# A Mamba mixing stage laid out with states and channels together on the partitions, the convolution moved to TensorE

## The chip, the cores and the metric

One core of one Trainium2 chip runs the kernel; seven cores stand idle. The metric is device time in microseconds (us) of one execution. The kernel before was timed three times, and one further execution was profiled.

## The reference, cut to what matters

Two residual layers over x [8, 512, 256]. Layer 0 (attention and experts) is not touched. Layer 1, for each of the 8 batches:

```python
xn = _layernorm(x, axis=-1)
x, z = split(einsum('bld,ed->ble', xn, in_proj_w))        # 512 channels each
u = silu(causal_conv_4_taps(x) + conv1d_b)
x_dbl = einsum('bld,rd->blr', u, x_proj_w)                # dt_low 16, B 16, C 16
delta = softplus(einsum('blr,dr->bld', dt_low, dt_proj_w) + dt_proj_b)
h[t] = exp(delta[t] * A) * h[t-1] + delta[t] * B[t] * u[t]      # 512 channels x 16 states
y[t] = sum_n(h[t] * C[t]) + u[t] * D_param
out = einsum('bld,ed->ble', y * silu(z), out_proj_w)
x = x + out + ffn(xn)     # ffn: 256x256 product, both sides rounded to a 6-bit grid in blocks of 32
```

## The kernel before

`route_block` and `attend_block` do layer 0. They end near 1025 us of the span and are the same in both kernels. `mix_block` does layer 1, and the whole change lies in it.

**The pieces.** The recurrence of a batch has 4 chunks of 128 channels (on the partitions), 16 states and 512 times. It is cut into 32 pieces; a piece is one chunk and two states, so a tile of 128x1024. Each piece q passes through four engines. ScalarE (ACT) makes the decays exp(delta*A) into one of three PSUM slots (`decay`, L1250, two instructions at L1257). GpSimd (POOL) makes the inputs B*du into one of `WS` = 6 slots of `work` (`drive`, L1148). VectorE (DVE) runs the scan in PSUM (`scan`, L1372) and multiplies the state of the piece before by C (`read`, L1378). TensorE (PE) adds the two halves of `work` into the bank of y with the identity as weights (`sum_states`, L1481).

**What holds what.** `decay` of piece n waits for `read` of piece n-3. `drive` of piece n waits until piece n-WS is summed, since it takes its slot:

```python
if n >= WS:
    pool.wait_ge(summed, n - WS + 1)
```

DVE's order is scan(q), the step work of q, read(q-1). PE's order at q is the step work of q, then the sum of piece q-1. At the end of a chunk, `gate_y` (L1386) multiplies y by silu(z) on DVE; it waits until PE has summed the whole chunk, and it stands behind the scan of pieces 1, 9, 17 and 25. `seed` (L1476) then opens the bank of y again with u*D.

**Step work of the next batch.** Between the pieces of batch b the engines prepare batch b+1. The constants `PE_AT`, `ACT_AT`, `DVE_AT` and `POOL_AT` (L62 to L67) name the piece at which each step stands. In their order: gather and weigh the expert rows (POOL, L1077, L1083), add them to x (L1088), layer norm (DVE L1327 to L1334, POOL L1092 to L1102), transpose (PE L1456), x half of the input projection (PE L1461), the last tap and the bias (ACT L1208), the other three taps (DVE L1363, in `convolve`), silu (ACT L1214), B, C and dt_low (PE L1467, ACT L1220), delta (PE L1471, ACT L1224 to L1231, POOL L1136 to L1140), z (PE L1461, ACT L1235, L1239), rounding to the grid (DVE L1341 to L1354, POOL L1111 to L1129), output projection of batch b-1 (PE L1489 to L1494, ACT L1247), cut in eight parts over pieces 2 to 9.

**The copies over the partitions.** B and C are rows of one partition each, wanted on all 128. SyncE's queue (SP) stores the 32 rows to memory (L1035) and loads them back as eight broadcasts of 1 MB, one for each pair of states (L1043). They are needed again only at the next batch, and each is loaded when the last piece of its kind is done.

## Time and profile before

| | |
|---|---|
| median of 3 runs | 2258.15 us (2257.34 to 2266.96) |
| profiled execution, its own time | 2259.47 us |
| its span, first to last instruction | 2257.7 us |
| TensorE clock granted, mean | 0.926 of 2.4 GHz |
| DVE, PE, POOL, ACT busy over the span | 1582.8, 1794.6, 1052.2, 963.1 us |

The span is 1.8 us shorter than the execution's own time. PE is the engine with the most busy time over the whole span, but layer 0 and layer 1 have different limits, so each is read for itself.

### The profile page before, as it was taken

The numbers are of one execution on the slowest core, as the hardware profiler recorded it, in microseconds if no ns is written. First come the engines' busy times: TensorE is split into PE (matmuls) and PEld (weight loads), VectorE is DVE, ScalarE is ACT, GpSimd is POOL, SyncE is SP. The second block draws the span as 40 slices with busy tenths as digits, with TensorE's granted clock in tenths as the row PEclk, the third lists the DMA queues.
The fourth block names the chain that finished last, engine by engine and source line by source line (L and its number), as shares of the span: only waits on it lengthen the run. The fifth ranks groups of instructions, "written<-read, shape, count | busy, mean of one in ns | idle before, by whom it ended". The sixth has DMA issues, their size and how long they took to land.

```text
span 2257.7 us, 20924 instructions
## 1 busy us (share of the span) xinstructions
PE 1794.6 (79%) x6312; PEld 844.5 (37%) x6312; DVE 1582.8 (70%) x1836; ACT 963.1 (43%) x1480; POOL 1052.2 (47%) x740
## 2 busy tenths in 40 slices
PE   7489899989899989894368877787777777877876
PEld 7253535353535353531123423433234233342333
DVE  6456464646464646452598898988979889889895
ACT  3125252626252525352437346364363643735532
POOL 2600000000000000004878959879598796896962
PEclk9899999999999999996689988999899998999999
DMA  5553536253526262602402204003031040210400
GB/s 179 205 80 109 92 101 100 101 96 106 93 98 103 94 107 94 107 10 82 159 0 81 98 1 159 19 32 128 19 142 37 1 158 19 99 70 2 149 10 9
DMA packets 84205, 189.13 MB, mean 84 GB/s; under 512 B 10561, under 2 KB 62914, under 8 KB 72370
## 3 DMA queue, kind: packets, MB, share of 16 engines
q1 hardware_dynamic: 81074, 180.07, 29.0%
q0 software_dynamic: 3072, 8.37, 1.2%
q8 instruction: 25, 0.41, 0.1%
q14 instruction: 34, 0.28, 0.0%
HBM read 151.72 MB, written 36.70 MB: 83 GB/s over the span
## 4 chain that ended last, share of the span: by engine, by line
DVE 14%; PE 11%; POOLq 11%; POOL 10%; issue 6%; ACT 1%; DVEq 1%; ACTq 0%
DVE ps L1372 6%; PE ps L1481 6%; DVE work L1378 3%; POOLq L1120 3%; POOL work L1148 3%; POOLq L1196 2%; POOL xn L1124 2%; PE ps L1461 2%; DVE u L1363 2%; POOLq L1139 2%; POOLq L1137 2%; PE ps L1489 2%; POOL e_rows L1122 1%; DVE absmax L1345 1%; POOL e_rows L1083 1%
## 5 line engine op out<-in xcount | busy, mean ns | idle before, releaser
L1481 PE MATMUL ps<-work,ident_sb 128*128 128x512 f32 x1024 | 548.0, 662 | 210.5 <-DVE work L1378 209.9
L1148 POOL TENSOR_TENSOR work<-bc,du 128x1024 f32<-128x1024 f32 x256 | 601.4, 2361 | 181.3 <-PE ps L1481 179.4
L1372 DVE TENSOR_TENSOR_SCAN ps<-ps,work 128x1024 f32<-128x1024 f32 x256 | 585.4, 2287 | 93.9 <-ACT ps L1257 50.4
L1257 ACT ACTIVATE ps<-delta,a_neg 128x512 f32<-128x512 f32 x512 | 331.7, 682 | 318.3 <-DVE work L1378 317.6
L699 DVE TENSOR_REDUCE m<-ps 128x1 f32<-128x512 f32 x512 | 327.3, 685 | 164.0 <-PE ps L805 162.3
L1481 PEld LDWEIGHTS ps<-work,ident_sb 128*128 128x128 f32 x1024 | 200.1, 208 | 500.0 <-DVE work L1378 321.1
L622 ACT ACTIVATE prob<-ps 128x1024 f32<-128x1024 f32 x256 | 256.8, 1021 | 234.5 <-PE ps L829 232.3
L1378 DVE TENSOR_TENSOR work<-ps,bc 128x1024 f32<-128x1024 f32 x256 | 308.4, 1205 | 0.0
L563 POOL TENSOR_TENSOR m_parts<-m,nil 128x16 bf16<-128x16 f32 x32 | 7.1, 221 | 604.2 <-DVE m L699 604.2
L805 PE MATMUL ps<-k_st,q_st 96*128 96x512 bf16 x512 | 184.5, 407 | 59.0 <-DMA k_st<-qk_parts 36.9
L1461 PE MATMUL ps<-xn_t,in_w 128*128 128x512 f32 x256 | 142.0, 688 | 54.0 <-DVE u L1363 35.1
L771 PE MATMUL ps<-rows_t,w 128*128 128x320 f32 x512 | 166.7, 470 | 4.3 <-ACT rows_t L600 4.3
L829 PE MATMUL ps<-q_st,k_st 99*128 99x512 bf16 x512 | 148.1, 383 | 0.1
L840 PE MATMUL ps<-prob,v 128*32 128x512 f32 x1024 | 139.8, 619 | 0.1
L577 POOL TENSOR_TENSOR att<-att,x_res 128x1024 f32<-128x1024 f32 x8 | 18.8, 2345 | 244.4 <-DVE att L684 244.4
L805 PEld LDWEIGHTS ps<-k_st,q_st 96*128 96x128 bf16 x512 | 48.1, 99 | 209.4 <-DVE m L699 137.1
L780 PE MATMUL ps<-w,hid 128*128 128x256 f32 x512 | 118.7, 382 | 5.9 <-ACT hid_rest L604 5.7
L771 PEld LDWEIGHTS ps<-rows_t,w 128*128 128x128 f32 x512 | 104.4, 208 | 46.7 <-issue 10.9
L671 DVE COPY e_out<-ps 128x256 f32<-128x256 f32 x32 | 12.0, 417 | 138.0 <-PE ps L780 138.0
L780 PEld LDWEIGHTS ps<-w,hid 128*128 128x128 f32 x512 | 95.8, 190 | 27.1 <-ACT hid_rest L604 11.2
L603 ACT ACTIVATE hid<-ps 128x256 f32<-128x256 f32 x128 | 49.2, 384 | 132.6 <-PE ps L771 132.6
L1461 PEld LDWEIGHTS ps<-xn_t,in_w 128*128 128x128 f32 x256 | 52.4, 214 | 135.2 <-issue 58.1
(168 smaller groups left out, 2045.3 us busy)
## 6 DMA issues: line engine op xcount, KB each, us to landing
bc<-bc_rows SPq DMA_DIRECT2D x64, 1024.0 KB, 4.7
w<-in_w SPq DMA_DIRECT2D x32, 1024.0 KB, 8.6
qk_parts<-parts SPq DMA_DIRECT2D x96, 128.0 KB
q_st<-qk_parts SPq DMA_DIRECT2D x96, 128.0 KB, 10.5
k_st<-qk_parts SPq DMA_DIRECT2D x96, 128.0 KB, 11.3
dispatch<-zeros SPq DMA_DIRECT2D x4, 1280.0 KB, 10.6
x_in<-in_x SPq DMA_DIRECT2D x8, 512.0 KB, 3.6
rows<-dispatch SPq DMA_DIRECT2D x32, 128.0 KB, 7.3
```

Source lines behind the costliest of these rows:

```text
L622: nc.scalar.activation(prob[:, n % PB, :, :], ps[:, ST[n % 2]:ST[n % 2] + 2, :], ACT.Exp, scale=SCALE).then_inc(prob_ready, 1)
L699: nc.vector.tensor_reduce(m[:, g % 2, qt, 2 * pair + i:2 * pair + i + 1], ps[:, S0 + i, :], AX.X, ALU.max).then_inc(s_reduced, 1)
L771: x = nc.tensor.matmul(ps[:, HIDE[i] + h % 2, 0:CAP], w1[:, i, k, h * P:(h + 1) * P], rows_t[:, k, :], start=(k == 0), stop=(k == KD - 1))
L780: x = nc.tensor.matmul(ps[:, E_OUT[i], j * DM:(j + 1) * DM], hid[:, h, j * P:(j + 1) * P], w2[:, i, h, :], start=(h == 0), stop=(h == HC - 1))
L805: nc.tensor.matmul(ps[:, S0 + i, :], q_st[0:STACK, h, qt * P:(qt + 1) * P], k_st[0:STACK, h, :], start=True, stop=True).then_inc(s_done, 1)
L829: x = nc.tensor.matmul(ps[:, ST[n % 2] + i, :], k_st[0:STACK + MROWS, h, kt * P:(kt + 1) * P], q_st[0:STACK + MROWS, h, :], start=True, st ...
L1148: nc.gpsimd.tensor_tensor(work[:, n % WS, :, :], bc[:, j, 0, :, :], du[:, b % 2, c, :].unsqueeze(1).broadcast_to([P, PAIR, SEQ]), ALU.mult ...
L1257: e = nc.scalar.activation(state(n)[:, i, :], delta[:, b % 2, c, :], ACT.Exp, scale=a_neg[:, c, PAIR * j + i:PAIR * j + i + 1])
L1372: nc.vector.tensor_tensor_scan(s, s, work[:, n % WS, :, :].rearrange("p i t -> p (i t)"), 0.0, ALU.mult, ALU.add).then_inc(state_ready, 1)
L1378: nc.vector.tensor_tensor(work[:, n % WS, :, :], state(n), bc[:, j, 1, :, :], ALU.mult).then_inc(read_ready, 1)
L1461: x = nc.tensor.matmul(ps[:, bank, :], in_w[:, k, col:col + P], xn_t[:, k, :], start=(k == 0), stop=(k == KD - 1))
L1481: x = nc.tensor.matmul(ps[:, YB, :], sb["ident"][:, :], work[:, n % WS, i, :], start=False, stop=(n % PAIRS == PAIRS - 1 and i == PAIR - 1))
```

## The change

A piece now holds 4 states times 32 channels on the partitions, for two blocks of 32 channels side by side: again 128x1024, again 32 pieces a batch, 8 to a chunk. delta and du of 32 channels must then stand on four groups of 32 partitions, so they are stored to memory and loaded back by SP (`store_inputs`, `load_inputs`); B and C need a quarter of the room. `sum_states` uses weights of 32 columns (`pick`, four stacked identities), so that each half of a piece goes to its own 32 output partitions. The convolution goes into the input projection: `tap_weights` multiplies the projection's weights by each tap once, and `in_proj_taps` adds 4 shifted products. Weighing and normalising go from POOL to ACT, two scalings of the grid go from POOL to ACT, `WS` falls from 6 to 4, and the steps get other places.

```diff
-PAIR = 2
-PAIRS = NS // PAIR
-PIECES = DC * PAIRS
-WS = 6
+CH = 32
+BLOCKS = P // CH
+QUADS = NS // BLOCKS
+PIECES = DC * QUADS * BLOCKS // 2
+PER_CHUNK = PIECES // DC
+WS = 4
 XS = 3
+US = 6
 RESET = 1e35
-GRID_STEPS = 5
+GRID_STEPS = 3
...
-PE_AT = {"out": 2, "w": 2, "first_quant": (3, 4), "turn_x": (10, 11), "x": (12, 13, 14, 15), "bc": 18, "dt": (19, 20, 21, 22),
+PE_AT = {"out": (1, 3), "w": 1, "first_quant": (3, 4), "turn_x": (6, 7), "x": (8, 10, 12, 14), "bc": 17, "dt": (19, 20, 21, 22),
          "z": (23, 24, 25, 26), "turn_quant": (27, 28)}
...
+ACT_AT = {"out": (4, 6), "w": 2, "first_quant": (4, 5), "weigh": 0, "normalise": 6, "turned": (8, 9), "x": (11, 13, 15, 17), "silu_u": 17,
+          "step": 13, "rows": 19, "dt": (21, 22, 23, 24), "softplus": 24, "z": (25, 26, 27, 28), "quant": (29, 30), "silu_z": 30}
+DVE_AT = {"statistics": 2, "max": 7, "binade": 10}
+POOL_AT = {"add": 1, "root": 5, "down": 10, "grid": 15, "up": 18, "gather": 20, "input": 27}
...
+                def load_quad(f, k):
+                    if f:
+                        sp.wait_ge(read_ready, f * PIECES - PER_CHUNK + 2 * k + 2)
+                    rows = io["bc"][f % 2].rearrange("(n r) t -> n (r t)", r=2)
+                    for i in range(QUADS):
+                        n = QUADS * k + i
+                        sp.dma_start(bc[i * CH:(i + 1) * CH, k, :, :].rearrange("p r t -> p (r t)"),
+                                     rows[n:n + 1, :].broadcast_to([CH, 2 * SEQ])).then_inc(bc_loaded[k], 16)
+
+                def store_inputs(f, c):
+                    sp.wait_ge(du_ready, f * DC + c + 1)
+                    sp.dma_start(io["rep"][f % 2, c], inputs[:, c, :, :].rearrange("p r t -> p (r t)")).then_inc(rep_stored[c], 16)
+
+                def load_inputs(f, c):
+                    sp.wait_ge(rep_stored[c], f * 16 + 16)
...
+                    for i in range(QUADS):
+                        sp.dma_start(rep[i * CH:(i + 1) * CH, c, :, :, :].rearrange("p j r t -> p j (r t)"),
+                                     io["rep"][f % 2, c].rearrange("(j p) x -> p j x", p=CH)).then_inc(rep_loaded[c], 16)
+
+                def spread(f):
+                    store_rows(f)
+                    store_inputs(f, 0)
+                    store_inputs(f, 1)
+                    load_inputs(f, 0)
+                    store_inputs(f, 2)
+                    load_inputs(f, 1)
+                    load_quad(f, 0)
+                    store_inputs(f, 3)
+                    load_quad(f, 1)
+                    load_inputs(f, 2)
+                    load_quad(f, 2)
+                    load_quad(f, 3)
+                    load_inputs(f, 3)
...
+                    if q % PER_CHUNK == 0:
+                        pool.wait_ge(rep_loaded[c], (b + 1) * QUADS * 16)
+                    if c == 0 and h == 0:
+                        pool.wait_ge(bc_loaded[k], (b + 1) * QUADS * 16)
                     if n >= WS:
                         pool.wait_ge(summed, n - WS + 1)
...
+                def scale_step(f):
+
+                    act.wait_ge(step_ready, f + 1)
+                    if f:
+                        act.wait_ge(rep_stored[DC - 1], f * 16)
+                    nc.scalar.activation(nudge, xn_step[:, :, :], ACT.Copy, scale=-2.0 ** -22)
+                    nc.scalar.activation(xn_step[:, :, :], xn_step[:, :, :], ACT.Copy, scale=1.5 * 2.0 ** 20).then_inc(step_scaled, 1)
...
-                    nc.vector.tensor_reduce(absmax[:, :], blocks(xn[:, :, :]), AX.X, ALU.max, apply_absolute_value=True)
+                    nc.vector.tensor_reduce(absmax[:, :, 0], blocks(xn[:, :, :]), AX.X, ALU.max, apply_absolute_value=True)
...
-                    nc.vector.tensor_scalar(xn_step, xn_step, 1.0, 4.0, ALU.max, ALU.min).then_inc(step_ready, 1)
-
-                def convolve(f, c, bank):
...
+                    cross = xn_step[:, :, :].rearrange("p t c -> p (t c)").rearrange("p (c i) -> p i c", i=2)
+                    nc.vector.tensor_scalar(cross, cross, 1.0, 4.0, ALU.max, ALU.min).then_inc(step_ready, 1)
...
+                def in_proj_taps(bank, c, done):
+
+                    for s in range(TAPS):
+                        for k in range(KD):
+                            x = nc.tensor.matmul(ps[:, bank, s:], in_x[:, k, TAPS - 1 - s, c * P:(c + 1) * P], xn_t[:, k, 0:SEQ - s],
+                                                 start=(s == 0 and k == 0), stop=(s == TAPS - 1 and k == KD - 1))
+                    x.then_inc(done, 1)
...
                     pe.wait_ge(read_ready, n + 1)
-                    for i in range(PAIR):
-                        x = nc.tensor.matmul(ps[:, YB, :], sb["ident"][:, :], work[:, n % WS, i, :],
-                                             start=False, stop=(n % PAIRS == PAIRS - 1 and i == PAIR - 1))
+                    for i in range(2):
+                        j = 2 * (n % 2) + i
+                        x = nc.tensor.matmul(ps[j * CH:(j + 1) * CH, YB, :], pick[:, :], work[:, n % WS, i, :],
+                                             start=False, stop=(n % PER_CHUNK >= PER_CHUNK - 2))
                     x.then_inc(summed, 1)
...
+                            for h in range(HALVES):
+                                if q == PE_AT["out"][h]:
...
+                                    out_proj(b - 1, h)
```

Before the first batch, POOL also gathers the expert rows of the second batch ahead of its `scale_input`, and PE waits for `tap_weights`. In the loop, PE's `in_proj_taps` of chunk c waits until ACT has taken chunk c-1 out of the bank (`in_taken`), and the output projection stands in two unbroken halves at pieces 1 and 3.

## Rows read from the trace of the kernel before

**Rows 1.** Page: busy times over the span.
```profile
PE 1794.6 (79%) x6312; PEld 844.5 (37%) x6312; DVE 1582.8 (70%) x1836; ACT 963.1 (43%) x1480; POOL 1052.2 (47%) x740
```

**Rows 2.** Busy time by stretch: length; PE, PEld, DVE, ACT, POOL; PEclk, DMA share, GB/s.
```profile
60.00:1024.00 964.00, 847.12 (x4000) 413.43 (x4000) 516.18 (x920) 382.64 (x641) 89.64 (x174) 0.95 0.44 99
1085.00:1090.00 5.00, 0.00 (x0) 0.00 (x0) 4.02 (x7) 2.82 (x2) 2.44 (x3) 0.50 1.02 431
1485.75:1631.43 145.68, 113.54 (x265) 48.76 (x264) 126.92 (x94) 69.74 (x100) 117.73 (x68) 0.92 0.19 69
```

**Rows 3.** Waits of DVE from 1140 us on: total, times, longest.
```profile
DVE ps L1372 <- ACT ps L1257: 49.1, 20, 4.0
DVE ps L1372 <- POOL work L1148: 31.3, 22, 2.6
DVE u L1363 <- ACT u L1208: 15.9, 14, 2.1
DVE sz L1386 <- PE ps L1481: 15.7, 17, 2.7
```

**Rows 4.** Timeline of DVE: start us, us, engine, line, operation, tiles, idle before.
```profile
1475.11 2.37 DVE L1363 SCALAR_TENSOR_TENSOR u<-ps,conv_w,u 128x509 f32<-128x509 f32 x3
...
1499.59 2.28 DVE L1372 TENSOR_TENSOR_SCAN ps<-ps,work 128x1024 f32<-128x1024 f32 x1
1502.90 2.28 DVE L1372 TENSOR_TENSOR_SCAN ps<-ps,work 128x1024 f32<-128x1024 f32 x1
...
1513.63 2.30 DVE L1372 TENSOR_TENSOR_SCAN ps<-ps,work 128x1024 f32<-128x1024 f32 x1 [4.01 <-ACT ps L1257]
```

**Rows 5.** Timeline of PE: 32-column tiles, sums, projection, an output half's ends.
```profile
400.45 1.06 PE L840 MATMUL ps<-prob,v 128*32 128x512 f32 x8
...
1478.66 3.11 PE L1481 MATMUL ps<-work,ident_sb 128*128 128x512 f32 x4 [3.04 <-DVE work L1378]
...
2100.15 1.88 PE L1481 MATMUL ps<-work,ident_sb 128*128 128x512 f32 x4
2101.86 1.88 PE L1461 MATMUL ps<-xn_t,in_w 128*128 128x512 f32 x4
...
2237.09 1.99 PE L1489 MATMUL ps<-out_w,sz 128*128 128x256 f32 x8 [0.79 <-DVE sz L1386]
...
2244.34 0.70 PE L1494 MATMUL ps<-x,ident_sb 128*128 128x256 f32 x2
```

**Rows 6.** Groups of POOL and ACT in one batch, 1485.75 to 1631.43 us.
```profile
L1148 POOL TENSOR_TENSOR work<-bc,du 128x1024 f32<-128x1024 f32 x32 | 74.9, 2357 | 23.0 <-PE ps L1481 22.7
L1124 POOL TENSOR_TENSOR xn<-xn,e_rows 128x1024 f32<-128x1024 f32 x3 | 7.1, 2355 | 0.5 <-issue 0.5
L1138 POOL TENSOR_TENSOR du<-delta,u 128x512 f32<-128x512 f32 x4 | 5.1, 1268 | 0.6
L1077 POOL DMA_INDIRECT e_rows<-expert_out,slot_cur x4 | 4.0, 999 | 1.6 <-issue 1.6
...
L1257 ACT ACTIVATE ps<-delta,a_neg 128x512 f32<-128x512 f32 x64 | 41.5, 682 | 37.1 <-DVE work L1378 36.9
```

**Rows 7.** Two lines of DVE, all their instructions: ns min/median/max.
```profile
L1345 DVE TENSOR_SCALAR absmax<-absmax x8: 180/4066/4586, 1053.4 to 2027.6; 128x32 f32<-128x32 f32 x8
...
L1354 DVE TENSOR_SCALAR e_rows<-e_rows x7: 693/2667/2673, 1194.0 to 2067.2; 128x1024 f32<-128x1024 f32 x7
```

**Rows 8.** Timeline of the stage's start.
```profile
1037.20 3.64 POOL L1083 TENSOR_SCALAR e_rows<-e_rows,gate_cur 128x256 f32<-128x256 f32 x4 [5.90 <-DMA e_rows<-expert_out,slot_cur]
...
1047.22 4.85 POOL L1102 TENSOR_SCALAR xn<-x,moments,rstd 128x256 f32<-128x256 f32 x4 [0.18 <-issue]
...
1054.87 16.29 PE L1461 MATMUL ps<-xn_t,in_w 128*128 128x512 f32 x32 [0.78 <-ACT xn_t L1203]
...
1087.91 1.26 POOL L1136 TENSOR_TENSOR delta<-delta,du 128x512 f32<-128x512 f32 x1 [2.42 <-ACT du L1231]
...
1100.47 2.34 POOL L1148 TENSOR_TENSOR work<-bc,du 128x1024 f32<-128x1024 f32 x1
```

More of the change, by code:

```diff
@@ L967, in mix_block @@
         fw_step = sz[:, 1, 1, :].rearrange("p (h c) -> p h c", h=2)
-        xn_step = e_rows[:, :, :].rearrange("p (h t) c -> p h (t c)", h=2)
+        xn_step = e_rows
+        conv_rows = work[:, 0:2, :, :].rearrange("p a i t -> p (a i) t")
+        nudge = inputs[:, DC - 1, :, :].rearrange("p r (t d) -> p (r t) d", d=DM)
+        delta, du = inputs[:, :, 0, :], inputs[:, :, 1, :]
         const_loaded = sem("const_loaded3")
@@ L1163, in _ @@
                 scale_up(0)
+                pool.drain()
+                place_gather(1)
+                gather(1, range(TT))
                 for c in range(DC):
@@ L1197, in _, with weigh_experts, normalise @@
                                 scale_input(f, c)
+                        if f + 1 < BATCH:
+                            if q == POOL_AT["gather"]:
+                                pool.drain()
+                                place_gather(f + 1)
+                                gather(f + 1, range(2))
+                            if q == POOL_AT["gather"] + 1:
+                                gather(f + 1, range(2, TT))
             @block.scalar
             def _(act):
+                def weigh_experts(f):
+                    act.wait_ge(e_gathered, (f + 1) * TT * 16)
+                    for t in range(TT):
+                        r = nc.scalar.activation(e_rows[:, t, :], e_rows[:, t, :], ACT.Copy, scale=gate_cur[:, t:t + 1])
+                    r.then_inc(e_weighed, 1)
+                def normalise(f):
+                    act.wait_ge(rstd_ready, f + 1)
+                    if f:
+                        act.wait_ge(quant_turned, f * KD)
+                    for t in range(TT):
+                        r = nc.scalar.activation(xn[:, t, :], x2[:, f % XS, t, :], ACT.Identity, scale=rstd[:, t:t + 1], bias=shift[:, t:t + 1])
+                    r.then_inc(xn_ready, 1)
                 def copy_turned(f, k, bank):
@@ L1303, in _ @@
                             silu_u(f)
-                        if q == ACT_AT["bc"]:
+                        if q == ACT_AT["step"]:
+                            scale_step(f)
+                        if q == ACT_AT["rows"]:
                             copy_rows(f, TB)
@@ L1362, in convolve, with tap_weights @@
+                def tap_weights():
+                    dve.wait_ge(const_loaded, CONSTS * 16)
+                    raw = in_x[:, :, TAPS - 1, :]
+                    for tap in range(TAPS):
+                        if tap == TAPS - 1:
                             dve.drain()
-                        r = nc.vector.scalar_tensor_tensor(u[:, f % 2, c, s:], ps[:, bank, 0:SEQ - s], conv_w[:, c, k:k + 1],
-                                                           u[:, f % 2, c, s:], ALU.mult, ALU.add)
@@ L1418, in _ @@
                 block_scale(0)
-                for c in range(DC):
-                    convolve(0, c, 2 + c)
                 binade(0)
```

286 lines of the change are left out of this document (132 added, 154 removed).

## The prediction

> **What bounds the kernel now.** I read the page first: over the whole span PE has the most busy time [rows 1], but the change lies in the second half. The busy time of one batch of the mixing stage says more [rows 2]: in 145.7 us DVE works 126.9, POOL 117.7 and PE 113.5. The timeline of DVE shows why: two scans follow each other after 3.31 us [rows 4], so 32 pieces are 106 us of every batch. The waits of DVE [rows 3] are what is left: in seven batches it waited 49.1 us for ACT's decays, 31.3 for POOL's drives, 15.9 and 15.7 in the convolution and the gate. DVE bounds the stage, with 18.8 us of waits a batch, and the reader should see that each other engine has time left on average. What counts is whether it delivers on time.
>
> **How much lateness the loop bears after the change.** With four slots in `work`, drive n starts when piece n-4 is summed, and takes 2.36 us [rows 6]. Read n-4 ends 0.1 after scan n-2 has begun. A sum then takes about 1.0: the 32-column tiles of the attention stage do four products side by side in 1.06 [rows 5], where the two of a piece now take 1.88 one after the other [rows 5]. So the sum is done 1.1 after scan n-2, and is needed 6.6-2.4 = 4.2 after it. The room is about 3 us; with hand-overs I use 2.8. Whatever stands on PE ahead of a sum, or on POOL beside its drives, costs DVE what exceeds it.
>
> **The terms of one period** (one batch; seven of eight have them, the last one in part).
>
> 1. DVE's own work. The convolution goes: 4 x 2.37 [rows 4] = 9.5. The scaling of 32 maxima takes 4.07 beside a working POOL and 0.18 at the stage's start, and the clamp of the steps 2.67 against 0.69 [rows 7]. Both now read with a stride of two. Nothing in the trace shows that form; the scaling can cost 0.18 to 4.07. I take 0.18, because only these forms, which take 0.69 for 1024 elements when left alone [rows 7], show the long times, and I expect the strided form to lose that pace: minus 3.9. The rule speaks against this. The Trainium skill, "Vector Engine (DVE) Microarchitecture Reference", section 5.1, lists for the mode with both ports a single source in SBUF and an even outer dimension, and no stride; by it the wait stays, and the total is 27 us more. DVE's work: 126.9-9.5-3.9 = 113.5.
>
> 2. Output projection in two unbroken halves. One half runs from 2237.09 to 2245.04 = 7.95 us [rows 5]. At piece 1 PE starts it after the gate, 2.9 us after the scan began, then come the seed 1.0, as two passes cost half of a pair [rows 5], and the sum of piece 0: done at 12.9, drive 4 at 15.3. DVE would be there at 12.1 (three pieces of 3.31, some 2.2 for the gate and the statistics): it waits 3.2. The second half at piece 3 does it again, 3.3. Together 6.5.
>
> 3. The taps on PE. A product of 128x512 is two passes of 0.43 (1.72 from one row to the next for four [rows 5]); `in_proj_taps` has 16, so 7.1 us with its tail, ahead of the sums 7, 9, 11 and 13. Block one starts 2.0 after scan 8 (ACT copies the transposes at 8 and 9), sum 7 is done at 10.3, and the gate behind scan 9 has stood since 6.2: 4.1. Block two waits until ACT, at its piece 11, has taken chunk 0: it starts 2.3 after scan 10, sum 9 ends at 10.5, drive 13 at 12.9, and DVE came at 11.7: 1.2. Blocks three and four: PE needs 7.1+2.3 for two pieces for which DVE needs 6.6: 2.8 each. Together 10.9.
>
> 4. POOL at 15 to 21: three grid steps and scaling up at 2.5 each with the drain, the gathers 5.6 [rows 6]. That is 15.6 beside seven drives that leave 0.95 each: 15.6-6.7-2.8 = 6.1. Gone are weighing and normalising; they stood where POOL had its room or waited already, so their going is in the new count, which replaces the old 31.3/7.
>
> 5. ACT: softplus keeps its 4.0 [rows 4]; the gate of piece 25 waits 1.2, as the z product ahead of sum 23 waits for ACT. The other ACT waits fall into those of 3 and 6. The steps that ACT takes over (eight of 128x256 and two of 128x1024, by its 682 ns for 512 [rows 6] some 5.5 us) fit between decays; it is busy 69.7 of 145.7 [rows 2]. If that cover is gone, they cost up to 5.
>
> 6. POOL at 27 to 30: four inputs of 2.9 (2 x 1.27 [rows 6] and drains) = 11.6, minus 5 x 0.95 and the room of 1.5 that the z products leave: 5.4.
>
> Terms 2 to 6 are waits of 34.1; the period without the next term is 147.6.
>
> 7. The reload, which is new. Drive 0 of a batch needs `rep` of chunk 0 and quad 0 of B and C, and ahead of them in SP's order stand the stores of chunks 0 to 2 and the loads of chunk 1. Counted from the second input (its store releases the first load): 1.05 MB of stores and 4.72 MB of loads. Whole-partition loads ran at 431 GB/s; the attention stage, whose loads fill few partitions, moved 99 GB/s at a share of 0.44, so 225 when full [rows 2]. The new loads fill 32 partitions each. Narrow: 21.0+2.4+1 for issue = 24.4; wide: 14.4. POOL itself needs 12.9 more for its remaining inputs and drives, and DVE has 0.9 of room. The wait is 1 to 11; I take 11, as the narrow row is the nearer one. The Trainium skill, "SBUF — State Buffer", Door 1, says 32 partitions reach 8 of 16 ports, 189 GB/s for 1 MiB, and that loads to different groups don't add up; by its rate the estimate is a wait of 15 and a total of 28 us more.
>
> Period: 158.6, against 145.7: +12.9, seven times = +90.
>
> **The start.** PE began the projection at 1054.9 and the first drive stood at 1100.5 [rows 8]. Weighing and normalising on ACT save 3.64+4.85 less about 3: 5 earlier. The taps add 48 passes: +20.6; the convolution they replace ran beside PE. `scale_step` ahead of delta: +2.4. POOL does grid and the second gather before its inputs, 15.6 after `scale_step` where ACT needs some 13: +2.6. Then the reload, with nothing beside it: the inputs start at 1108.5, the second ends at 1114.3, +24.4 gives 1138.7: 38 later; wide 28.
>
> **The last batch** has term 2 and a shorter last sum: +5.5.
>
> **The sum:** 90+38+5.5 = 133 on the profiled 2259.5 us; the median stands 1.3 lower: **2391 us**. Unknown as well: the clock. The granted clock was 0.92 in a batch [rows 2]. A sum took 3.11 behind a PE wait of 3.04, and 1.88 behind other products [rows 5]: the lower level, 1.2 of 2.4 GHz. PE now works a third of each quiet piece; if all four late blocks (two halves, the first taps, z) start so, 1.2 each is 34 in total. I put in 0, the value of blocks that follow each other, and keep 34 for the range. This case alone spans 2310 to 2440.
>
> **The rivals.**
> - **The blocks are hidden, and DVE's saving comes through (faster).** Against it is the step-by-step count above; for it, PE's total falls, to 113.5-32 x 0.9+20.6 = 105 a period, so there is room on average. It decides at one place: the sum behind a block of taps must be done by 4.2 us after scan n-2. Then ACT and POOL waits stay at 7.0 and 4.5 [rows 3] and the reload at 1: 126.0 a period, 7 x -19.7 = -138, start +28: **2150 us**.
> - **The loads run at the wide rate.** Everything else as above: -70-10: **2311 us**. Against it is the row at 0.44.
> - **The two 32-column products don't overlap.** A sum stays at 1.88, and each of six blocks lets go 0.9 later: +40: **2431 us**. Against it is the row of 1.06, though that one has four tiles; for it, that none has two.
> - **Savings and blocks cancel.** Wide loads, and POOL's terms half hidden: near 2260.
>
> **How the numbers follow.** Forecast with its own bounds 0.50, wide loads 0.14, no overlap 0.08, cancelling 0.08, hidden blocks 0.20. I read a difference of over 0.5% (11 us) as one that measurement can tell. Faster 0.20, and of the cancelling case most is same: 0.05; slower 0.75. The range leaves out most of the faster case and a little at the top: 2240 to 2445.
>
> **What would show it.** Right: DVE's scans wait for POOL's drives after pieces 3, 5, 12, 14 and 16, and POOL for PE; the gate of piece 9 waits 4 us; the first drive of each batch waits for a DMA on `rep` or `bc` by about 10; the sum of a piece takes about 1.0; the first scan stands near 1141. Wrong: a period near 126 with no DMA wait at the seam, a scaling of maxima still at 4, or sums at 1.9.

## The result and the profile after

The changed kernel takes **2435.41 us** (median of 4 runs, 2432.92 to 2437.33) against 2257.74 us of the kernel before on the same chip (2256.93 to 2266.96): a ratio of 1.078, 95% interval 1.076 to 1.080. It is 178 us slower. The prediction had 2391 us in a range of 2240 to 2445, and slower at 0.75: direction and range held, and 44 us are missing.

The page after, first the busy times of the span, then the row of the copies (KB each, median us from issue to landing):

```profile
PE 1817.2 (75%) x6696; PEld 770.0 (32%) x6696; DVE 1505.5 (62%) x1744; ACT 1001.6 (41%) x1542; POOL 941.8 (39%) x676
...
rep<-rep_rows SPq DMA_DIRECT2D x128, 512.0 KB, 16.0
```

Against [rows 1], DVE and POOL did less (77 and 110 us), PE 23 us more. No engine is nearer to its limit than it was, so the 178 us are waits. One batch by itself, and two stretches in which the loads ran (columns as in [rows 2]: length; PE, PEld, DVE, ACT, POOL; PEclk, DMA share, GB/s):

```profile
1637.36:1800.50 163.14, 112.13 (x312) 38.47 (x312) 118.07 (x81) 75.21 (x108) 104.14 (x61) 0.79 0.37 88
1613.00:1618.00 5.00, 1.92 (x4) 0.19 (x4) 3.05 (x3) 2.56 (x3) 4.58 (x5) 0.50 1.04 208
1643.00:1655.00 12.00, 11.39 (x43) 7.40 (x43) 9.99 (x14) 4.36 (x7) 3.48 (x2) 0.83 1.04 216
```

DVE's work fell by 8.9 us a batch (126.92 to 118.07) and the batch grew from 145.7 to 163.1. What DVE waited for, from 1140 us on, answers to [rows 3]:

```profile
DVE ps L1440 <- POOL work L1181: 282.4, 86, 38.3
DVE sz L1454 <- PE ps L1555: 42.4, 15, 3.6
DVE ps L1440 <- ACT ps L1316: 36.2, 13, 5.0
```

Waits for ACT fell from 49.1 to 36.2 and those of the convolution (15.9) are gone. Waits for the gate rose from 15.7 to 42.4, waits for POOL's drives from 31.3 to 282.4. Of these, 38.3 lie ahead of the first scan, which here comes after 1140 us and in the kernel before came ahead of it; like is compared with like at 31.3 and 244.1. The timeline of DVE in one batch shows where the drives are late: at the first scan, at piece 4, at piece 6, from 15 to 21 and from 29 on; the gate of piece 9 is the one that waits for PE.

```profile
1637.36 2.30 DVE L1440 TENSOR_TENSOR_SCAN ps<-ps,work 128x1024 f32<-128x1024 f32 x1 [13.59 <-POOL work L1181]
...
1657.65 2.30 DVE L1440 TENSOR_TENSOR_SCAN ps<-ps,work 128x1024 f32<-128x1024 f32 x1 [4.57 <-POOL work L1181]
...
1666.55 2.30 DVE L1440 TENSOR_TENSOR_SCAN ps<-ps,work 128x1024 f32<-128x1024 f32 x1 [2.17 <-POOL work L1181]
...
1676.70 2.16 DVE L1414 TENSOR_SCALAR absmax<-absmax 128x32 f32<-128x32 f32 x1
...
1685.12 0.69 DVE L1454 TENSOR_TENSOR sz<-ps,sz 128x512 f32<-128x512 f32 x1 [2.56 <-PE ps L1555]
...
1689.05 1.98 DVE L1420 TENSOR_SCALAR e_rows<-xn 128x1024 int32<-128x1024 int32 x1
...
1708.90 2.30 DVE L1440 TENSOR_TENSOR_SCAN ps<-ps,work 128x1024 f32<-128x1024 f32 x1 [2.59 <-POOL work L1181]
```

And the timeline of POOL across the seam of two batches (the place where one batch's pieces end and the next one's begin). It finishes its last drive at 1620.25 and stands for 14.66 us until the first drive of the next batch, which needs the new `rep` and `bc`. Its drive at 1706.43 is that of piece 15; it waited for PE, and the scan at 1708.90 for it:

```profile
1617.91 2.34 POOL L1181 TENSOR_TENSOR work<-rep,bc 128x1024 f32<-128x1024 f32 x1
1634.92 4.64 POOL L1181 TENSOR_TENSOR work<-rep,bc 128x1024 f32<-128x1024 f32 x2 [14.66 <-issue]
...
1676.47 2.35 POOL L1181 TENSOR_TENSOR work<-rep,bc 128x1024 f32<-128x1024 f32 x1 [2.87 <-PE ps L1555]
...
1688.14 2.34 POOL L1181 TENSOR_TENSOR work<-rep,bc 128x1024 f32<-128x1024 f32 x1 [0.62 <-PE ps L1555]
...
1706.43 2.36 POOL L1181 TENSOR_TENSOR work<-rep,bc 128x1024 f32<-128x1024 f32 x1 [4.64 <-PE ps L1555]
```

PE in the same batch: the first part of an output half behind a long wait, the sums of pieces 0 and 1 together, the first block of taps, the sum of one piece, a later block, again the sums of two pieces together, and a z product. A product of a piece is two passes, so a sum of one piece is x4 and of two x8.

```profile
1640.83 1.92 PE L1555 MATMUL ps<-work,pick 128*32 128x512 f32 x4 [15.08 <-DVE work L1446]
1643.61 3.63 PE L1563 MATMUL ps<-out_w,sz 128*128 128x256 f32 x8 [0.86 <-DVE sz L1454]
...
1649.20 1.89 PE L1563 MATMUL ps<-out_w,sz 128*128 128x256 f32 x8
...
1653.99 1.07 PE L1555 MATMUL ps<-work,pick 128*32 128x512 f32 x8
...
1676.30 7.78 PE L1532 MATMUL ps<-xn_t,in_taps 128*128 128x512 f32 x16
1684.02 1.05 PE L1555 MATMUL ps<-work,pick 128*32 128x512 f32 x4
...
1698.25 7.11 PE L1532 MATMUL ps<-xn_t,in_taps 128*128 128x512 f32 x16 [0.89 <-ACT u L1254]
1705.29 1.07 PE L1555 MATMUL ps<-work,pick 128*32 128x512 f32 x8
...
1746.70 3.78 PE L1525 MATMUL ps<-xn_t,in_z 128*128 128x512 f32 x4 [0.66 <-ACT inputs L1284]
```

The start, which answers to [rows 8]: the projection with its taps on PE, the first input on POOL and the first drive, which comes 21.68 us after the last input, when a load of `bc` has landed. The first scan follows at 1152.0.

```profile
1054.38 30.35 PE L1532 MATMUL ps<-xn_t,in_taps 128*128 128x512 f32 x64 [0.73 <-issue]
...
1115.86 1.26 POOL L1167 TENSOR_TENSOR inputs<-inputs 128x512 f32<-128x512 f32 x1 [2.07 <-issue]
...
1149.55 4.64 POOL L1181 TENSOR_TENSOR work<-rep,bc 128x1024 f32<-128x1024 f32 x2 [21.68 <-DMA bc<-bc_rows]
```

**Where the 178 us lie**, by the times of the first scan of each batch: the first scan of all stands at 1152.0 instead of 1102.9 (+49.1); the first period is 157.9 instead of 145.8 (+12.1); the next six average 163.3 instead of 145.5 (+106.8); the last batch is 7.4 longer. Sum 175.4, against 2433.1 - 2257.7 = 175.4 of the spans of the two profiled executions.

### The profile page after: what moved, and what is told of

Same layout as the page of the kernel before. It is cut to its first block, busy times and chain, and to the rows that moved or that the text cites. A ratio compares the mean times of both kernels' runs of the same rounds, so it can differ in the third digit from the quotient of the medians.

```text
span 2433.1 us, 21744 instructions
## 1 busy us (share of the span) xinstructions
PE 1817.2 (75%) x6696; PEld 770.0 (32%) x6696; DVE 1505.5 (62%) x1744; ACT 1001.6 (41%) x1542; POOL 941.8 (39%) x676
## 4 chain that ended last, share of the span: by engine, by line
PE 14%; issue 11%; DVE 10%; POOL 7%; POOLq 7%; DMA 5%; ACT 1%; DVEq 1%; SPq 1%; ACTq 0%
DVE ps L1440 6%; PE ps L1532 4%; POOL work L1181 4%; DMA rep<-rep_rows 3%; PE ps L1563 3%; DVE work L1446 3%; PE ps L1555 2%; POOLq L1152 2%; POOLq L1221 1%; POOL xn L1156 1%; PE ps L1565 1%; PE ps L1525 1%; DMA bc<-bc_rows 1%; POOLq L1168 1%; POOLq L1170 1%
## 5 line engine op out<-in xcount | busy, mean ns | idle before, releaser
L1440 DVE TENSOR_TENSOR_SCAN ps<-ps,work 128x1024 f32<-128x1024 f32 x256 | 586.3, 2290 | 318.7 <-POOL work L1181 282.4
L1181 POOL TENSOR_TENSOR work<-rep,bc 128x1024 f32<-128x1024 f32 x256 | 599.3, 2353 | 441.4 <-PE ps L1555 314.2
L1555 PE MATMUL ps<-work,pick 128*32 128x512 f32 x1024 | 325.9, 792 | 362.1 <-DVE work L1446 362.0
L1316 ACT ACTIVATE ps<-rep,a_neg 128x512 f32<-128x512 f32 x512 | 332.4, 681 | 640.2 <-DVE work L1446 599.0
L1532 PE MATMUL ps<-xn_t,in_taps 128*128 128x510 f32 (+3 forms) x512 | 235.1, 615 | 13.4 <-ACT u L1254 12.4
L1555 PEld LDWEIGHTS ps<-work,pick 128*32 128x32 f32 x1024 | 37.9, 121 | 590.9 <-DVE work L1446 526.9
L1532 PEld LDWEIGHTS ps<-xn_t,in_taps 128*128 128x128 f32 x512 | 98.5, 197 | 156.5 <-issue 113.8
L580 POOL TENSOR_TENSOR att<-att,x_res 128x1024 f32<-128x1024 f32 x8 | 18.8, 2346 | 244.4 <-DVE att L687 244.4
L783 PEld LDWEIGHTS ps<-w,hid 128*128 128x128 f32 x512 | 95.8, 190 | 27.1 <-ACT hid_rest L607 11.2
L1525 PE MATMUL ps<-xn_t,in_z 128*128 128x512 f32 x128 | 82.4, 782 | 27.2 <-ACT sz L1294 23.1
```

The costliest lines, as they stand in the source:

```text
L783: x = nc.tensor.matmul(ps[:, E_OUT[i], j * DM:(j + 1) * DM], hid[:, h, j * P:(j + 1) * P], w2[:, i, h, :], start=(h == 0), stop=(h == HC - 1))
L1181: nc.gpsimd.tensor_tensor(work[:, n % WS, :, :], rep[:, c, 2 * h:2 * h + 2, 1, :], bc[:, k, 0, :].unsqueeze(1).broadcast_to([P, 2, SEQ]), ...
L1316: e = nc.scalar.activation(state(n)[:, i, :], rep[:, c, 2 * h + i, 0, :], ACT.Exp, scale=a_neg[:, c, 2 * h + i, k:k + 1])
L1440: nc.vector.tensor_tensor_scan(s, s, work[:, n % WS, :, :].rearrange("p i t -> p (i t)"), 0.0, ALU.mult, ALU.add).then_inc(state_ready, 1)
L1532: x = nc.tensor.matmul(ps[:, bank, s:], in_x[:, k, TAPS - 1 - s, c * P:(c + 1) * P], xn_t[:, k, 0:SEQ - s], start=(s == 0 and k == 0), sto ...
L1555: x = nc.tensor.matmul(ps[j * CH:(j + 1) * CH, YB, :], pick[:, :], work[:, n % WS, i, :], start=False, stop=(n % PER_CHUNK >= PER_CHUNK - 2))
```

## The experiments

Each kernel was timed beside the kernel before on its own chip (2255.9 to 2260.0 us there). "Period" is the time from one first scan to the next in the middle batches.

### Two edits of the seam

`e1_order`: SP issues quads 0 and 1 of B and C, which the first drives need, ahead of the loads of `rep`.

```diff
                     store_inputs(f, 0)
+                    load_quad(f, 0)
                     store_inputs(f, 1)
+                    load_quad(f, 1)
                     load_inputs(f, 0)
                     store_inputs(f, 2)
                     load_inputs(f, 1)
-                    load_quad(f, 0)
+                    load_quad(f, 2)
                     store_inputs(f, 3)
-                    load_quad(f, 1)
                     load_inputs(f, 2)
-                    load_quad(f, 2)
                     load_quad(f, 3)
```

> Only SP's order changes: quads 0 and 1 of B and C stand ahead of the loads of chunk 0, no byte more or less. In the changed kernel rep of chunk 0 had landed 12.7 us before quad 0, behind which the 2 MB of chunk 1 stood. Theory (queue order at the narrow rate): the wait of DVE at the seam falls from 13.4 to 3 or 4 us a batch, the kernel from 2435 to about 2355. Rival (the loads as a whole are too slow): the wait moves to the pieces behind the seam, and the time falls by less than 25.

Measured: 2357.63 us, ratio 1.043 (1.041 to 1.045), 78 us less than the changed kernel. The first scan of all stands at 1141.7, periods are 151 to 154, and the wait at the seam is 1.6 to 2.9 us. The loads themselves ran no faster (16.4 us to landing against 16.0); two of them only stood in the wrong place.

`e2_wide`: each load of a group fills every fourth partition instead of 32 neighbours; `pick`, the layout of `a_neg` and the quads follow.

```diff
-                        sp.dma_start(bc[i * CH:(i + 1) * CH, k, :, :].rearrange("p r t -> p (r t)"),
+                        sp.dma_start(bc[i::QUADS, k, :, :].rearrange("p r t -> p (r t)"),
...
-                        sp.dma_start(rep[i * CH:(i + 1) * CH, c, :, :, :].rearrange("p j r t -> p j (r t)"),
+                        sp.dma_start(rep[i::QUADS, c, :, :, :].rearrange("p j r t -> p j (r t)"),
```

> The same four loads of 512 KB per chunk in the same order, but each fills every fourth partition (channel by channel, the four states next to each other) in place of 32 neighbours. Theory (the partitions reached set the rate): the rate at full share rises from about 212 GB/s to about 420, the seam wait falls to 1 or 2 us, the kernel comes to about 2340. Rival (32 partitions are slow wherever they lie): no change, 2435.

Measured: 2363.38 us, ratio 1.045 (1.043 to 1.048). The wait at the seam is 2.9 to 4.9 us. A stretch in which the loads ran, and their row of the page:

```profile
1744.00:1759.00 15.00, 3.91 (x10) 0.44 (x12) 8.36 (x7) 4.32 (x9) 9.11 (x6) 0.50 1.02 411
```
```profile
rep<-rep_rows SPq DMA_DIRECT2D x128, 512.0 KB, 6.7
```

Same bytes, same share of the DMA engines, 411 GB/s instead of 208 to 216, and 6.7 us to landing instead of 16.0. The mechanism is shown; I had put the gain 23 us too high.

`e8_order_wide`: both edits.

> The changed kernel with both edits of the seam together, e1 and e2. Each alone left 1.6 to 4.9 us of the seam's wait of 13.4. If they remove the same wait, the two together give 2340 to 2355 us, hardly more than e1 alone (2357.6); if the loads still hold up other things (the start, where the loads of all chunks must land before scans 0, 8 and so on), the start falls by another 8 us and the last of the seam by 1 to 2 us a batch: 2325 to 2340.

Measured: 2327.04 us, ratio 1.032 (1.030 to 1.033). The seam's wait is gone from batch 1 on, the first scan stands at 1138.8, periods are 148 to 150.5. So the seam and the longer start that comes from the same loads were 108 us of the 178. The other waits of a batch stand where they were and as long (4.57 at piece 4, 2.17 at 6, 2.57 at the gate of 9), so this part adds up by itself. Of the 67 us by which the span still exceeds that of the kernel before (2324.9 against 2257.7), 36 lie ahead of the first scan, 24 in the seven periods and 7 in the last batch.

### Shorter blocks on TensorE

`e3_short_blocks`: the output projection in four parts (pieces 1, 2, 4, 5) and the taps in eight.

```diff
-PE_AT = {"out": (1, 3), "w": 1, "first_quant": (3, 4), "turn_x": (6, 7), "x": (8, 10, 12, 14), "bc": 17, "dt": (19, 20, 21, 22),
+PE_AT = {"out": (1, 2, 4, 5), "w": 1, "first_quant": (3, 4), "turn_x": (6, 7), "x": (8, 10, 12, 14), "bc": 17, "dt": (19, 20, 21, 22),
...
-                                    in_proj_taps(TB, c, in_done)
+                                    in_proj_taps(TB, c, in_done, (0, 1))
+                                if q == PE_AT["x"][c] + 1:
+                                    in_proj_taps(TB, c, in_done, (2, 3))
```

> The output projection stands in four parts at pieces 1, 2, 4, 5, the taps in eight parts at pieces 8 to 15, the same products. Theory (a block is paid for what it exceeds the room of 2.8 us): DVE's waits at pieces 4 and 6 fall from 6.7 to about 1, at the gate of piece 9 from 2.6 to 1, at 15 to 17 they stay near 4 since PE lacks time there altogether: about 56 us less, 2380. Rival (PE's total is what counts, not the length of a block): less than 10 us.

Measured: 2426.59 us, ratio 1.074 (1.071 to 1.078): 9 us less, not 55. The waits from 1140 us on:

```profile
DVE ps L1440 <- POOL work L1181: 240.0, 84, 38.2
DVE ps L1440 <- ACT ps L1316: 84.9, 34, 4.5
```

POOL's share fell by 42 us and ACT's rose by 49, with new waits for decays of 2.7 at piece 7 and 3.5 at 18. Halving PE's blocks moved the lateness to another engine. The medians differ by 9 us, and single executions of this kernel spread from 2423 to 2435.

### The strides undone

`e4_plain_forms`: the maxima and the clamp of the steps are read without a stride of two, as in the kernel before.

> Only the two strides of two are undone (scaling of the maxima, clamp of the steps). In the changed kernel the scaling took 2.16 us beside a working POOL, the clamp 0.70. Theory (the stride doesn't matter, what POOL does beside it does): the scaling stays at 2.2, the clamp at 0.7, the time is the same. Rival (the stride had halved the wait): the scaling is back at 4.07, the kernel 13 us slower.

Measured: 2437.20 us, ratio 1.079 (1.077 to 1.081), no difference. The scaling of the maxima, all its instructions (ns min/median/max), in this kernel and in the changed one:

```profile
L1414 DVE TENSOR_SCALAR absmax<-absmax x8: 183/2149/2156, 1052.2 to 2167.8; 128x32 f32<-128x32 f32 x8
```
```profile
L1414 DVE TENSOR_SCALAR absmax<-absmax x8: 182/2156/2157, 1053.0 to 2168.2; 128x32 f32<-128x32 f32 x8
```

The stride is nothing. Of what it is instead, see the unexpected, below.

### The convolution back on VectorE, then the slots

`e5_conv_dve`: `tap_weights` and the shifted weights go; TensorE multiplies the plain weights, ACT applies the last tap, DVE adds the other three in pieces 11 to 14, and the places of the projection and of silu move with it (not among the lines below).

```diff
-                    for s in range(TAPS):
-                        for k in range(KD):
-                            x = nc.tensor.matmul(ps[:, bank, s:], in_x[:, k, TAPS - 1 - s, c * P:(c + 1) * P], xn_t[:, k, 0:SEQ - s],
-                                                 start=(s == 0 and k == 0), stop=(s == TAPS - 1 and k == KD - 1))
+                    for k in range(KD):
+                        x = nc.tensor.matmul(ps[:, bank, :], in_x[:, k, c * P:(c + 1) * P], xn_t[:, k, :], start=(k == 0), stop=(k == KD - 1))
...
+                            for c in range(DC):
+                                if q == DVE_AT["convolve"][c]:
+                                    convolve(f, c, TB)
```

> One part of the change undone: the causal convolution goes back to VectorE (three operations a chunk, at pieces 11 to 14), and TensorE multiplies the plain input weights once instead of four shifted weights. My theory (the sum of the prediction, in which each block on TensorE is paid by VectorE as a wait of its readout): the gate wait at piece 9 (2.56 us) and the share of the taps in the waits at 15 to 18 (5 us) go, about 7.5 us; VectorE gets back the 9.5 us of the convolution and a wait or two for ScalarE between its shifts; the period stays at 163 to 166 us. At the start the 5.5 us of tap weights and some 20 us of TensorE's 30 go, and 10 of VectorE come. Time 2415 to 2440 us. Rival: the taps delay more than the sum says, since they also make the slots of work come free late for GpSimd far behind them; then the period falls under 160 us and the time under 2405.

Measured: 2430.03 us, ratio 1.077 (1.075 to 1.079); periods 165 to 169, the first scan at 1127.0. With four slots this part of the change, made for DVE's sake, comes out even, and the trace shows two halves of that: the taps on PE shorten the seven periods by 2.9 us each, 20 in all, and lengthen the start by 25.0 (1152.0 against 1127.0). In the batch from 1621.89 the wait at the gate of 9 and those at pieces 15 to 19 are gone; 0.8 and 2.6 at pieces 20 and 21 remain.

`e6_conv_dve_ws6`: the same with the slots back, which fit again.

```diff
-WS = 4
+WS = 6
```

> As e5, and six slots of work instead of four (they fit because the four shifted weights are gone). Only this differs from e5. My theory: the waits of the readout for GpSimd at pieces 4, 6, 15 to 21 and 29 to 31 are a matter of slack: with four slots GpSimd can stand at most two pieces ahead of the readout, so each block of its own work of 4 to 8 us is paid in part. With two slots more of slack (3.5 us each) these 15 to 20 us shrink to 5 to 8; period 151 to 154 us, time 2325 to 2350. Rival: GpSimd's own total (104 us of work and its gaps) or TensorE sets the pace and slots change only where the wait stands: within 1% of e5.

Measured: 2320.19 us, ratio 1.029 (1.027 to 1.031): **110 us for two slots**. The waits of e5, then those of e6:

```profile
DVE ps L1441 <- POOL work L1181: 203.4, 54, 13.3
DVE ps L1441 <- ACT ps L1316: 41.2, 20, 5.0
```
```profile
DVE ps L1441 <- ACT ps L1316: 73.0, 28, 5.0
DVE ps L1441 <- POOL work L1181: 54.4, 9, 7.8
```

Nearly all waits for POOL at pieces 4, 6, 15 to 21 and 29 to 31 are gone, with POOL doing the same work (943.0 and 941.5 us over the span); only the seam is left (7.4 instead of 13.3). In their place ACT became the late engine. Some 40 of the 110 us are the shorter wait at the seven seams, so this gain and the 108 us of e8 overlap and must not be added. What two slots are worth beside the taps on PE no run shows, since they don't fit beside the shifted weights.

`e9_before_ws4`: the kernel before with four slots.

```diff
-WS = 6
+WS = 4
```

> The kernel before with one edit: four slots of work instead of six. The change took two slots away to make room for its shifted weights; e6 gave them back to the changed kernel (its convolution undone) and won 110 us. If the price is one of slack alone and not of the new mix, the kernel before must lose about as much when it is cut to four: GpSimd's blocks between its pieces, which now cost VectorE few waits, are paid in part, 10 to 15 us a batch, time 2330 to 2370 us. Rival: slots matter only for the new mix, whose GpSimd blocks (grid, scale, inputs) lie otherwise, or because the output and taps on TensorE are what they bridge: within 1.5% of before, under 2290.

Measured: 2312.10 us, ratio 1.022 (1.019 to 1.026): 52.6 us, between theory and rival. Waits of DVE:

```profile
DVE ps L1372 <- POOL work L1148: 110.2, 69, 2.8
DVE absmax L1341 <- POOL xn L1102: 25.5, 7, 3.7
DVE ps L1372 <- ACT ps L1257: 23.0, 14, 2.5
```

Against [rows 3], the waits for POOL rose by 79 us, a new one of 25.5 came for POOL's normalising, and half of ACT's went, as the decays had time while DVE stood for POOL. So slack is worth something in both kernels, and twice as much in the new mix. Some 40 us of the 110 lie at the seam, where the kernel before has no reload of `rep`; that longer blocks on PE are the rest of the difference is likely, and not shown.

### All of it, and the start

`e7_all`: e6 with both edits of the seam and the output projection in four parts.

> e6 with the two edits of the seam (the quads ahead of the loads of chunk 0, and each load over every fourth partition) and the output projection in four parts. What is left of the new mix is the layout itself and TensorE's sum of each piece. Theory: the seam of 13.6 us falls to 2 or 3 and the output halves' 6.7 to 2; period 138 to 142 us, the start some 45 us earlier than in e6 minus what the start's convolution costs; time 2215 to 2260 us, about level with the kernel before. Rival: VectorE, now at 127 us of work a batch, and the ScalarE waits that came up in e3 (2.7 us at 7, 3.5 at 18) keep the period at 147 or more: 2290 or more. It beats the kernel before by over 0.5% only under 2248.

Measured: 2302.51 us, ratio 1.021 (1.019 to 1.023). The rival was right. The first scan moved up to 1115.0, but the period stayed at 150.

```profile
DVE ps L1441 <- ACT ps L1316: 90.2, 35, 5.3
DVE u L1432 <- ACT u L1253: 25.9, 21, 1.4
DVE ps L1441 <- POOL work L1181: 22.9, 7, 3.6
```

POOL is late at the seam only (3.3 us a batch); the decays are late, behind the second output copy (5.3 at piece 7), behind softplus (5.0 at 25) and in the chain of the convolution.

`e11_tap_weights_late`: the changed kernel, with the weights of the taps made behind the first statistics.

```diff
-                tap_weights()
                 dve.wait_ge(a_exp, 1)
...
                 statistics(0)
                 aggregate(0)
+                tap_weights()
```

> The changed kernel with one edit at its start: VectorE makes the four shifted weights behind the first statistics instead of ahead of them. In the changed kernel they are 5.5 us on VectorE ahead of the statistics of batch 0, on the chain to the first scan, which my sum had left out. Theory: the first scan comes 4 to 6 us earlier and nothing else moves: 2429 to 2432 us. Rival: the taps on TensorE then wait for the weights instead, and nothing is won: 2434 to 2437.

Measured: 2433.64 us, ratio 1.077 (1.073 to 1.080). In the profiled execution the first scan stands 3.9 us earlier (1148.1) and the span is 3.9 shorter (2429.2); the medians differ by 1.8 us, which these runs can't tell from nothing. The mechanism shows in the trace, its worth doesn't in the times.

### ScalarE's work taken apart

`e10_retimed`: e6 plus both edits of the seam, and the logarithm of softplus a piece behind its exponential, the second output copy at 7, the chunks of the convolution two pieces apart.

```diff
-PE_AT = {"out": (1, 3), "w": 1, "first_quant": (3, 4), "turn_x": (6, 7), "x": (10, 11, 12, 13), "bc": 17, "dt": (19, 20, 21, 22),
+PE_AT = {"out": (1, 3), "w": 1, "first_quant": (3, 4), "turn_x": (6, 7), "x": (9, 10, 12, 14), "bc": 17, "dt": (19, 20, 21, 22),
...
-ACT_AT = {"out": (4, 6), "w": 2, "first_quant": (4, 5), "weigh": 0, "normalise": 6, "turned": (8, 9), "x": (11, 12, 13, 14), "silu_u": 16,
+ACT_AT = {"out": (4, 7), "w": 2, "first_quant": (4, 5), "weigh": 0, "normalise": 6, "turned": (8, 9), "x": (11, 12, 14, 16), "silu_u": 17,
...
-DVE_AT = {"statistics": 2, "max": 7, "convolve": (11, 12, 13, 14), "binade": 10}
+DVE_AT = {"statistics": 2, "max": 7, "convolve": (11, 12, 14, 16), "binade": 10}
...
+                        if q == ACT_AT["softplus"] + 1:
+                            softplus_log(f)
```

> e6 plus both edits of the seam (not the output in four parts, which only moved the wait from piece 4 to ScalarE's at 7), and ScalarE's work taken apart, since in e6 and e7 it is its decay that comes late: the logarithm of softplus one piece behind its exponential, the second output copy behind the decay of piece 7, and the convolution's chunks two pieces apart from the second on. Waits of e7 a batch: 5.3 at 7, 3.8 at 12 to 14, 5.0 and 2.8 at 25, 3.4 at 0. Theory: these shrink by 9 to 12 us, period 139 to 142 us, time 2230 to 2255 us, level with or just under the kernel before. Rival: the lateness of ScalarE is TensorE's (it waits for matmuls at the lower clock) and splitting moves it elsewhere: period 146 or more, 2275 or more.

Measured: 2231.73 us, ratio 0.986 (0.982 to 0.990), periods 138.5 to 141.6. The waits for ACT's decays fell to 10 us in all; the gate of piece 25 now waited 4.5 to 6.1 for PE:

```profile
1648.96 0.69 DVE L1460 TENSOR_TENSOR sz<-ps,sz 128x512 f32<-128x512 f32 x1 [4.49 <-PE ps L1563]
```

`e12_z_apart`: TensorE's second z product leaves piece 24.

```diff
-         "z": (23, 24, 25, 26), "turn_quant": (27, 28)}
+         "z": (23, 25, 26, 27), "turn_quant": (28, 29)}
...
-          "step": 13, "rows": 19, "dt": (21, 22, 23, 24), "softplus": 24, "z": (25, 26, 27, 28), "quant": (29, 30), "silu_z": 30}
+          "step": 13, "rows": 19, "dt": (21, 22, 23, 24), "softplus": 24, "z": (25, 27, 28, 29), "quant": (30, 31), "silu_z": 31}
```

> e10 with one edit: TensorE's second z product leaves piece 24 (z at 23, 25, 26, 27 and its followers a piece later). In e10 VectorE waits 4.5 to 6.1 us a batch for the sums of TensorE at the gate of piece 25, because TensorE stands at piece 24 in front of the z product, waiting 2.7 us for ScalarE to take the one before, with the sum that the gate needs behind it. Theory: the gate's wait falls to 1 us or less, the period from 139.5 to 135.5 or 136.5, the time to 2200 to 2215 us. Rival: TensorE reaches the gate late anyway (its products at the lower clock, 2 us each, from piece 19 on), or the seam's wait grows by what is won, since the z of the next batch and its inputs come later: 2225 to 2235 us.

Measured: **2208.13 us**, ratio 0.979 (0.977 to 0.980), faster than both kernels. A middle batch, and the waits from 1140 us on:

```profile
1518.89:1655.98 137.09, 93.23 (x264) 31.37 (x264) 127.67 (x93) 75.96 (x110) 104.42 (x61) 0.79 0.29 104
```
```profile
DVE ps L1446 <- POOL work L1181: 34.4, 16, 3.5
DVE ps L1446 <- ACT ps L1318: 18.1, 10, 2.5
```

DVE works 127.7 of 137.1 us: as much work as before the change [rows 2], in a period 8.6 shorter. The gate's wait is gone in all batches but at the kernel's end. What this version keeps of the change is the layout with its reload, the sums in columns of 32, the output projection in halves and the steps moved from POOL to ACT; the convolution on TensorE is not in it. The kernel before was not retimed in the same manner, so how much of the gain belongs to the layout stays open.

## Why the prediction was right, and what was mis-sized

Its terms for one period beside the batch shown above (1637.36 to 1800.50):

| term | predicted | measured |
|---|---|---|
| 1 DVE's own work | 113.5 | 118.1 |
| 2 output halves | 3.2 + 3.3 | 4.57 + 2.17 |
| 3 and 4, taps and POOL's blocks | 10.9 + 6.1 | 2.56 (gate 9), 8.6 (15 to 21) |
| 5 softplus and gate 25 | 5.2 | 8.1 |
| 6 POOL at 27 to 30 | 5.4 | 5.7 |
| 7 reload | 11 | 13.6 |
| period | 158.6 | 163.1 |

The waits sum to 45.2 where 45.1 was predicted, though not each in its place: terms 3 and 4 came out 5.8 too large and terms 5 and 7 5.5 too small. That the sum agrees to 0.1 is luck. Of the 42 us that the spans are longer than forecast, 29 lie in the seven periods, 11 in the start and 2 in the last batch.

- **Term 1 failed, by 4.6 us a batch** (some 32 us in seven). It took 3.9 off for the stride, on the ground that the scaling of the maxima would lose its long form. The scaling took 2.16, not 0.18, and e4 shows that the stride does nothing: 2.0 of the 4.6. The mask (the row at 1689.05), 0.68 in the batch before, took 1.98: another 1.3. The convolution's twelve operations were worth 8.9 by their busy time and not 9.5; the last 0.7 is open. The rule that I had set aside was right in kind: the Trainium skill, "Vector Engine (DVE) Microarchitecture Reference", section 5.1, names no stride among the conditions, and the wait stayed, at half its length. That the +27 us worked out by it lies near 32 is chance, since the scaling is 14 of the 32. Nor did the scaling and the mask lengthen the batch by what they took. The gate of piece 9 waited for PE at any rate, and waited 2.56 where 4.1 was forecast; scan 13, where 1.2 was forecast, came 12.7 us after scan 10 and not 11.7, by when its drive had just ended. The clamp went the other way: 2.67 in four of the seven batches before, 0.70 in all of them after.
- **Term 2** was right in size: the halves stand in 6.7 instead of 6.5. The first is longer, as PE had waited 15.08 us and its first eight products took 3.63 instead of 1.89 (the granted clock was 0.50 from 1631.0 to 1640.8, the level of 1.2 GHz). The second is shorter, since the sums of pieces 0 and 1 went out together, eight passes in 1.07 us.
- **Terms 3 and 4** were 5.8 too large together. Each tap block took the 7.1 us of the count (7.78 behind a wait). The gate of piece 9 waited; at 13 nothing did, as said under term 1; scan 15 waited 2.59 where 2.8 was forecast, for a drive that had waited 4.64 for the sum behind the third block. Behind the fourth block, forecast at 2.8, drive 17 did not wait for PE: POOL was still in its own steps. Two delays that run side by side had been added. PE also caught up sooner, since two sums went out together (the row at 1705.29): from the third block to the fourth it took 8.0 us where 9.4 was forecast. The prediction had a price for one sum only (1.05 measured against 1.0). By e5, in which the taps are gone, 7.8 of the 11.2 us hang together with the taps and 3.4 with POOL's own steps, against 10.9 and 6.1. That split is an estimate, as DVE's convolution stands there in their place.
- **Term 5** was 2.9 too small. 1.4 us stand at piece 22, where it had none. The gate of 25 waited 2.9 instead of 1.2, behind two z products; the four passes of the one at 1746.70 took 3.78 us and not 1.88 as in [rows 5].
- **Term 7** was right in kind: at full share the loads moved 208 and 216 GB/s in the two stretches shown, by the row of the attention stage 225, and e2 shows that the partitions each load fills are the cause. It came out at 13.6 where 11 stood. From the end of the second input to the first drive it took 27.7 us and not 24.4; the lower rate is 0.9 to 1.7 of the 3.3, an estimate from 4.72 MB, and the rest is open. The Trainium skill, "SBUF — State Buffer", Door 1, gives 189 GB/s for 32 partitions and a wait of 15 was worked out by it; the wait lies between the two, and the rates of the two stretches agree with the page's larger figure for that span, about 218. In single stretches of 5 us in which stores or quads of B and C moved too, the rate was up to 290.
- **The start** had +38 and gave +49.1. The first input came at 1115.9 where 1108.5 stood. Missing was `tap_weights`, 5.5 us on DVE ahead of the first statistics (e11 gives 3.9 of them back); the other 3.5 are open. From the second input to the first drive it took 27.8 us (1121.7 to 1149.55), not 24.4. The last batch had 5.5 and gave 7.4.
- **The clock** stood at 0: the mean granted clock fell from 0.926 to 0.838. PE's work shows it behind waits, and also in a whole stretch of each batch, in which it was granted 0.57:

```profile
1731.00:1760.00 29.00, 24.23 (x39) 4.77 (x40) 19.37 (x12) 20.01 (x26) 18.24 (x11) 0.57 0.06 19
```

What the first output half and the gate of 25 waited beyond their forecast is 3.0 us a batch, 21 in seven. This is an estimate of the clock's price, inside the 34 that the range had kept for it. No run changes the clock alone, so it isn't shown. e12 runs at 0.845 and is faster than the kernel before; a low clock does not by itself undo the gain.

**The signs.** DVE waited behind pieces 3, 5 and 14 as said, not behind 12; behind 16 it waited for POOL's own steps. A sum took 1.05, and 1.9 at the lower level. The scaling was neither at 0.18 nor at 4, and the first scan stood at 1152 and not 1141.

**The rivals.** Hidden blocks was wrong: outside the seam DVE waited 31.6 us a batch, where that rival had 11.5. Wide loads was wrong for this kernel (208 and 216 GB/s), and that two products of 32 columns would not overlap was wrong too (1.05 us for a piece). Against "room on average" stands e6: with four slots POOL may be two pieces ahead of DVE, and what is longer is paid. That a block is paid for what exceeds the room is only half of it, though: e3 halved PE's blocks, and of 55 us expected 9 came back, since ACT was late next.

**DVE's saving came, and waits outweighed it**: its work fell by 8.9 us a batch and its waits rose from 18.8 to 45.1. The loads account for 108 us (e8). Two slots are worth 110 (e6 against e5), of which some 40 lie in the same seam. Both are side effects, of the new layout and of the room that the shifted weights took. The sum had the four slots in it as its room of 2.8 us, but never asked what two more were worth.

## What to carry to other kernels

Before giving up slots to make room for a cheaper computation, price the slots alone: here the convolution on TensorE won 20 us in seven periods and lost 25 at the start (e5 without it is 5 us faster), and the two slots that its weights displaced were worth 110 in the kernel without it. A copy that is new in the loop should be asked for twice, by its order in the queue and by the partitions each transfer fills; either edit took some 75 us off. When one engine's lateness is removed the next one's shows (POOL, then ACT, then PE), so retime in small steps, each read from the longest wait of the last: from e7 to e12, which also puts the output projection back into halves, that took 94 us off.

## What the runs showed of the hardware that was not expected

**A TENSOR_SCALAR of DVE waits for POOL's drives to end.** In the changed kernel the scaling of 32 maxima ran from 1676.70 to 1678.86 and POOL's drive from 1676.47 to 1678.82 (both rows above). The mask, 0.68 us in the kernel before, ran from 1689.05 to 1691.03 beside a drive that ended at 1690.48. In the kernel before it took 4.07 us, until POOL's run of four drives ended (1594.57 and 1594.52):

```profile
1585.26 9.26 POOL L1148 TENSOR_TENSOR work<-bc,du 128x1024 f32<-128x1024 f32 x4
...
1590.50 4.07 DVE L1345 TENSOR_SCALAR absmax<-absmax 128x32 f32<-128x32 f32 x1
```

In e9 POOL stood still at that place, and the same instruction took 0.18:

```profile
1614.95 0.18 DVE L1345 TENSOR_SCALAR absmax<-absmax 128x32 f32<-128x32 f32 x1
...
1616.57 2.35 POOL L1148 TENSOR_TENSOR work<-bc,du 128x1024 f32<-128x1024 f32 x1 [3.98 <-PE ps L1481]
```

The Trainium skill, "SBUF — State Buffer", "Who interferes with whom", says that such a DVE operation and a GpSimd operation take a shared pair of ports whole, and that the second to come stands until the first is done. The trace agrees for a single drive. Behind the run of four, the scaling came in the third drive (some 2.3 us each) and stood until the fourth was done, one instruction longer than the rule names.

**Products of 32 columns for different output partitions overlap across instructions of different pieces**: the two products of one piece took 1.05 us, the four of two pieces 1.07, when PE had two sums to catch up on. A late PE catches up faster than its single sum tells.

**Loads over every fourth partition run at nearly twice the rate of loads over 32 neighbours** (411 against 208 to 216 GB/s), but take longer to issue: one load took SP 606 ns in e2 and 432 in the changed kernel (medians of 128).
